# Attention opening of a fused kernel: two queues for the first heads' rows, four buffers for the first values, six pairs three slots sooner, ones in pieces

## The reference

```python
# attention: 16 heads of 16, causal, no bias
q, k, v = Wq x, Wk x, Wv x            # x after layernorm
attn = softmax(where(causal, q k / sqrt(16), -inf))
x = x + layernorm(Wo (attn v))
# mixture of experts: 8 experts, 2 of them per token
logits = router x + bias              # x after layernorm
gate, up = split(gate_up x + bias)    # 512 each
act = (clip(up) + 1) * min(gate, 7) * sigmoid(1.702 min(gate, 7))
x = x + layernorm(sum over 2 experts of weight * (down act + bias))
```

## Time and profile before

| | before |
|---|---|
| median of 3 runs | 2109.95 us (2108.41 to 2113.77) |
| the profiled execution | 2107.62 us, of which span 2105.9 |
| TensorE busy | 1964.5 us, 93% |
| VectorE busy | 1588.1 us, 75% |
| ScalarE busy | 1338.4 us, 64% |
| GpSimd busy | 948.3 us, 45% |
| granted TensorE clock, mean | 0.975 |

### The profile page before, as it was taken

The page is one execution under the profiler, slowest core; times in us unless marked ns, Lnnn a source line. Parts: engine busy times, 40 slices in busy tenths (PEclk is TensorE's granted clock), DMA queues, the critical chain, the costliest instruction groups (busy, mean ns, idle before and its releaser), DMA issues. The chain is left out here.

```text
span 2105.9 us, 50512 instructions
## 1 busy us (share of the span) xinstructions
PE 1964.5 (93%) x13630; PEld 1301.5 (62%) x13631; DVE 1588.1 (75%) x5427; ACT 1338.4 (64%) x3413; POOL 948.3 (45%) x1442
## 2 busy tenths in 40 slices
PE   6799999999999999999999999999999999999970
PEld 4334444444444444444433349999999999999970
DVE  2877788888888888887888827778767777777757
ACT  3377777777777777777777675555444444444436
POOL 5233344455646556456455563455323333333327
PEclk9799999999999999999999999999999999999995
DMA  7533546464454635545355368889788888887867
GB/s 210 184 112 126 176 156 199 134 208 160 155 167 138 193 126 168 164 138 180 118 171 182 113 205 255 234 246 252 219 249 256 259 261 256 256 258 234 242 183 319
DMA packets 259201, 413.99 MB, mean 197 GB/s; under 512 B 37056, under 2 KB 195264, under 8 KB 251840
## 3 DMA queue, kind: packets, MB, share of 16 engines
q1 hardware_dynamic: 219392, 367.28, 53.1%
q0 software_dynamic: 29824, 35.54, 9.6%
q10 hardware_dynamic: 9792, 8.93, 1.4%
HBM read 288.64 MB, written 122.41 MB: 195 GB/s over the span
## 5 line engine op out<-in xcount | busy, mean ns | idle before, releaser
L1013 ACT ACTIVATE arena<-ps_e 128x512 f32<-128x512 f32 (+3 forms) x1536 | 687.3, 493 | 276.4 <-PE ps_e L1233 260.0
L648 DVE CUSTOM_DVE_ANT_0 arena<-ps_s,c 128x128 bf16<-128x128 f32 (+3 forms) x1024 | 479.1, 481 | 61.0 <-PE ps_s L1214 57.1
L1214 PE MATMUL ps_s<-arena 96*128 96x512 bf16 (+3 forms) x1536 | 489.3, 334 | 25.4 <-DMA arena<-qk_parts 7.1
L1233 PE MATMUL ps_e<-arena 98*128 98x512 bf16 (+3 forms) x1536 | 483.2, 329 | 2.9 <-ACT arena L1013 2.0
L651 DVE TENSOR_REDUCE cmax<-ps_s 128x1 f32<-128x512 f32 x512 | 351.2, 686 | 142.7 <-PE ps_s L1214 132.5
L1367 PE MATMUL ps_s<-arena 128*128 128x128 f32 x3296 | 405.2, 276 | 6.5 <-DMA arena<-in_gate_up 4.9
L1367 PEld LDWEIGHTS ps_s<-arena 128*128 128x128 f32 x3296 | 394.3, 192 | 19.1 <-DMA arena<-in_gate_up 7.9
L1214 PEld LDWEIGHTS ps_s<-arena 96*128 96x128 bf16 x1536 | 152.1, 101 | 356.7 <-DVE cmax L648 91.5
L1252 PE MATMUL ps_o<-arena 128*32 128x512 f32 (+3 forms) x3072 | 329.9, 502 | 4.9 <-ACT ot L1027 3.5
L545 POOL TENSOR_SCALAR_AFFINE_SELECT arena<-arena 128x512 f32<-128x512 f32 x256 | 162.9, 636 | 294.8 <-ACT arena L1013 294.4
L529 POOL DMA_INDIRECT acc<-blank,place_now x136 | 216.2, 1590 | 132.0 <-POOL place_now L524 67.6
(11 more groups left out here) (179 smaller groups left out, 2796.9 us busy)
## 6 DMA issues: line engine op xcount, KB each, us to landing
arena<-in_gate_up SPq DMA_DIRECT2D x138, 1024.0 KB
arena<-qk_parts SPq DMA_DIRECT2D x384, 128.0 KB, 2.9
qk_parts<-space SPq DMA_DIRECT2D x120, 192.0 KB
d_xin<-xs SPq DMA_DIRECT2D x141, 130.5 KB
v_aug<-space SPq DMA_DIRECT2D x32, 512.0 KB, 4.9
arena<-v_aug SPq DMA_DIRECT2D x32, 512.0 KB
o_t<-ot SPq DMA_DIRECT2D x64, 256.0 KB, 2.0
c_x<-in_x SPq DMA_DIRECT2D x34, 256.0 KB, 5.4
```

The lines of the kernel that those rows point to most:

```text
L648: dve.tensor_tensor_reduce(summed[:, m % RJ, 0:w], ps_s[:, m % RS, 0:w], after[:, HALF - w:HALF], 1.0, LOWEST, ALU.add, ALU.max, dst).then ...
L1013: act.activation(pw[:, n % RP, 0:w], ps_e[:, n % RE, 0:w], ACT.Exp, scale=SCALE).then_inc(e_done, 1)
L1214: pe.matmul(ps_s[:, m % RS, 0:w], qs[0:ROWS, slot, i * P:(i + 1) * P], ks[0:ROWS, slot, k0:k0 + w], start=True, stop=True).then_inc(s_scor ...
L1233: pe.matmul(ps_e[:, n % RE, 0:w], ks[0:ROWS_M, slot, j * P:(j + 1) * P], qs[0:ROWS_M, slot, q0:q0 + w], start=True, stop=True).then_inc(e_ ...
```

## The change

Four edits. The rows of quad 0 are issued by SyncE (q) and ScalarE (k), both in slot `BEGIN`; all quads' rows now go q first, then k. Pairs 2 and 3 get value buffers of their own in the arena, which VectorE fills with ones beforehand. The first pairs are placed in earlier slots. The two rows of ones are filled in three pieces, one per quad buffer.

| slot of | before | after |
|---|---|---|
| turning of pairs 0 to 5 | -36, -33, -30, -27, -23, -16 | -39, -36, -33, -30, -27, -20 |
| values copy of pairs 0 to 5 | -22, -21, -20, -19, -17, -10 | -27, -26, -25, -24, -21, -14 |
| `qk_parts` store of pairs 0 to 5 | -29, -26, -23, -20, -16, -9 | -32, -29, -26, -23, -17, -13 |
| load of x for pairs 4 to 7 | -31, -28, -24, -17 | -34, -31, -28, -21 |
| value stores of pairs 0 to 3 | -18 | -18 |
| ones | -18 | -20, -12, -9 |
| pair 6 and later | | the same |

```diff
-    A_AT = [BEGIN - 18 + 3 * a for a in range(EARLY)] + [BEGIN - 5, BEGIN + 2] + [NE * (a - 6) - 4 for a in range(6, PAIRS)]
-    V_AT = [BEGIN - 4 + a for a in range(EARLY)] + [start + 6 for start in A_AT[EARLY:]]
+    A_AT = [BEGIN - 21 + 3 * a for a in range(EARLY + 1)] + [BEGIN - 2] + [NE * (a - 6) - 4 for a in range(6, PAIRS)]
+    V_AT = [BEGIN - 9 + a for a in range(EARLY)] + [start + 6 for start in A_AT[EARLY:]]
...
+        def vout_of(a):
+            if 2 <= a < EARLY:
+                return arena[:, 13312 + (a - 2) * 1024:13312 + (a - 1) * 1024].rearrange("p (s c h d) -> p s c h d", s=4, c=2, h=4)
+            return vout[:, a % 2]
...
+        def load_rows(engine, quad, w):
+
+            b, s, u = quad // 4, quad % 4, quad % SETS
+            for nth, part in enumerate(((0, 0, 0, 1, 1, 2), (0, 1, 2, 0, 1, 0))[w]):
+                engine.dma_start((qs, ks)[w][nth:ROWS:ROWS // DH, u * 4:u * 4 + 4].rearrange("r h t -> r (h t)"),
+                                 qk_v[b, w, s // 2, s % 2, part]).then_inc(loads[u], 16)
...
-                for a in pairs_due(7, 9, g):
+                for a in due([max(start + (7 if a < FIRST_EVEN else 9), BEGIN + 1 if a >= EARLY else SLOTS.start) for a, start in enumerate(A_AT)], 0, g):
...
                 if g == BEGIN:
                     for u in range(2):
                         sp.wait_ge(qk_out[u], EARLY // 2 * Q_STORES * 16)
-                    load_heads(0)
+                    load_rows(sp, 0, 0)
                     for a in range(EARLY):
                         store_values(a)
...
-                if g == BEGIN:
-                    pool.wait_ge(a_p3, 2 * EARLY + 1)
-                    pool.memset(ks[ROWS:ROWS_M], -1.0).then_inc(ones, 1)
-                    pool.wait_ge(ones, 1)
+                for u, (at, done_by, n) in enumerate(((BEGIN - 2, a_p3, 2 * EARLY + 2), (BEGIN + 6, a_p3, 2 * EARLY + 4), (BEGIN + 9, s_mlo, 2))):
+                    if g == at:
+                        pool.wait_ge(done_by, n)
+                        pool.memset(ks[ROWS:ROWS_M, u * 4:u * 4 + 4], -1.0).then_inc(ones, 1)
+                        pool.wait_ge(ones, u + 1)
...
-            dve.memset(vout, 1.0).then_inc(v_ones, 1)
+            dve.memset(vout, 1.0)
+            dve.memset(arena[:, 13312:15360], 1.0).then_inc(v_ones, 1)
...
+                if g == BEGIN:
+                    for u in range(2):
+                        act.wait_ge(qk_out[u], EARLY // 2 * Q_STORES * 16)
+                    load_rows(act, 0, 1)
...
                             act.wait_ge(a_v, a + 1)
-                            if a >= 2:
+                            if a >= EARLY:
                                 act.wait_ge(v_out[u], a // 2 * 16)
...
-                    pe.wait_ge(ones, 1)
+                    pe.wait_ge(ones, SETS)
```

More of the change, by code:

```diff
@@ L323, in load_heads @@
             def load_heads(quad):
[L325 to L333, removed]
+                load_rows(sp, quad, 0)
+                load_rows(sp, quad, 1)
             def load_values(quad):
@@ L341, in store_values @@
                 sp.dma_start(v_aug[b, :, :, 2 * j:2 * j + 2].rearrange("s p c h d -> p s (c h d)"),
-                             vout[:, u].rearrange("p s c h d -> p s (c h d)")).then_inc(v_out[u], 16)
+                             vout_of(a).rearrange("p s c h d -> p s (c h d)")).then_inc(v_out[u], 16)
             def slots(j):
@@ L1106, in _ @@
                             for t in range(2):
-                                last = act.activation(vout[:, u, :, t, :, 0:DH],
+                                last = act.activation(vout_of(a)[:, :, t, :, 0:DH],
                                                       bank[:, t * D:(t + 1) * D].rearrange("p (s h d) -> p s h d", s=4, h=4), ACT.Copy)
```

## The result

| | before | after |
|---|---|---|
| median of 4 runs | 2110.01 us (2108.41 to 2113.77) | 2131.98 us (2128.35 to 2135.08) |
| the profiled execution | 2107.62 us, span 2105.9 | 2128.35 us, span 2126.6 |
| granted TensorE clock, mean | 0.975 | 0.970 |

The ratio is 1.0101, with a 95% interval of 1.0083 to 1.0119: the change costs 22 us (17.5 to 25). That is slower, as forecast, but 13 us more than the 2119 forecast and 5 above the range's end.

A forecast was written before the change was run, and what follows sets the result against it. The opening, with its 13 us gap before the head phase, was taken to shift everything behind it; +11.7 and -1.5 make +10.2, giving 2117.8 from the profiled execution or 2120.1 from the median, taken as 2119 us, range 2110 to 2127.

The forecast's parts named there:

- Steps 1 to 3: Opening before the head rows: TensorE 2.7 us late, pair 3's store landed at 46.8, SyncE's rows from 48.0, 6.1 later.
- step 2: Pair 3's store: ScalarE's second part done at 41.1, third part at 42.3 instead of 37.4, landed at 46.8.
- step 3: SyncE before its head rows: pair 7's x waits for pair 5's normalising at 47.6; rows start at 48.0, not 41.91.
- Step 4: ScalarE's copy of pair 4's values waits for the stores of pairs 0 and 2, until 58.0, ahead of its row loads.
- Step 5: ScalarE's six rows: issued from 60.3 over 3.2 us, landing 2.8 later; first score 66.3 against 51.74, bounds 62.9 to 70.
- The rule weighed in step 5: ScalarE's rows: a second issuing engine saves only initiation time, the 16 DMA engines being shared; at most some 3.4 us gained.
- Step 6: Head phase: VectorE starts at 66.6, 11.7 us later than 54.9; the phase of 43.1 us gets 1.5 shorter.
- rival C: No change: short value landings, cheap ScalarE issues, a head phase losing its 6.7 us idle; +1 to +4, 2110; chance 0.10.
- The sum: Whole kernel: +11.7 us for the later start and -1.5 in the head phase give +10.2.
- A: Intended gain: values wait and half the issues go, rows land at 47.9; -8.2 us, 2099 to 2102, say 2100; chance 0.08.
- B: Partial delay: SyncE starts near 42 to 43 but ScalarE still waits at its copy; +5 us, 2114; chance 0.12.
- The sign that had 0.78: Whole kernel: slower by over 0.3% (6.3 us) given 0.78, faster 0.09, within 0.3% 0.13.

The follow-up runs named there:

- e8: The kernel before with the four value buffers alone (rows q before k, one queue, old slots): 2106.71 us, ratio 0.9997.
- e12: The kernel after with value stores of pairs 0 to 3 one slot behind each copy and all quad 0 rows on SyncE: 2114.21 us, ratio 1.0024.
- e2: The kernel after with all twelve rows of quad 0 on SyncE: 2117.99 us, ratio 1.0053.
- e3: The kernel after with the value stores of pairs 0 to 3 one slot behind each copy, still two queues: 2114.52 us, ratio 1.0039.
- e4: The kernel after with SyncE waiting for all of quad 0 before issuing the rows of quads 1 and 2: 2124.29 us, ratio 1.0081.
- e7: The kernel after with old slots and ones in one piece, value stores issued only when quad 0 has landed: 2108.23 us, ratio 0.9997.
- e5: The kernel after with 28 unused matmuls on TensorE before the first score: 2124.90 us, ratio 1.0078.
- e1: The kernel after with the slots of before and the ones in one piece; two queues and four buffers stay: 2110.38 us, ratio 1.0018.
- e6: The kernel before with only the ones filled in three pieces: 2108.57 us, ratio 1.0005.
- e10: The kernel before with four value buffers, 36 unused matmuls and pair 7's x loaded right behind the value stores: 2104.07 us, ratio 0.9986.

## Why the prediction was right in kind and wrong in size

The runs make a ladder to the exponent score: before 98.2; four buffers 96.1 (e8); the new slots with the ones in pieces, the stores early and one queue 101.5 (e12, 5.4 us more); the stores back in slot -18, so that ScalarE waits and TensorE with it, 108.4 (e2, 6.9 more); the k rows put behind that wait 116.2 (after, 7.8 more). The second queue costs nothing where ScalarE is not held (e3, 101.0) and 7.8 us where it is.

**Steps 1 to 3** held: GpSimd finished pair 3's third part at 42.95 (forecast 42.3), and SyncE's rows began at 47.18 (48.0). Some of this nearness is luck: ScalarE was done with the second part at 40.1 and not 41.1, but GpSimd had pair 5's scale and shift ahead of the third part, which step 2 left out, and began it at 41.8. The load of x for pair 7, which step 3 had as the last wait, was not it: issued at 46.27 in 0.37 us, it left 0.5 us in which SyncE waited on, by its order for the stores of pair 3 (forecast landed at 46.8). The slots without the wait cost 5.1 us at the first score (e12's 57.2 against e8's 52.1), where these steps had 6.1 for the start of the rows.

**Step 4** held: the wait was there, in one piece of 11.30 us, on pair 2's store, released at 57.55 (58.0). 15.2 of the 18.0 us hang on it (e3): 6.9 by the wait with no row behind it (e2 against e12), and the rest by the rows behind it.

**Step 5** failed at its last term, the time of ScalarE's six rows beside SyncE's. ScalarE began at 59.47, 0.8 us before the forecast 60.3. Its six issues then spread over 4.7 us and not 3.2, and the landing behind them took 6.5 us and not 2.8: the first score at 70.7 and not 66.3, past the upper bound of 70 as well. The forecast had nothing for SyncE's passing rows and its upper bound 1.5 us; they took 5.2 (70.7 - 59.5 - 3.2 - 2.8), and e4, which removes just these rows, has the landing of 2.7 us back. The bound took these loads at 369 GB/s; with the engines full they passed at 225 to 262. The rule weighed in step 5 (the Trainium skill, DMA: Bandwidth & Descriptors, "Issuing engines are not separate DMA queues") agrees with these traces: e7 and e3 have the first score within 0.5 us of their counterparts with one queue (e8 and e12). I had used it to cap a gain and not to price the loss of a load that must share the engines with one that has time.

**Step 6** failed in its sign for the head phase: -1.5 us forecast, +1.9 measured (43.3 to 45.2, just over the 45 us that the prediction named as its test). It had pair 5's work in the first slots at half clock and set no loss for it. In the first 16 us behind the first row maximum the granted clock is 0.65 where the kernel before has 0.80, and VectorE gets 10.7 us of work done instead of 12.8. e5 shows the clock to cost 4.0 us: with the unused matmuls the phase from the first score is 41.5 us. A long stand of TensorE does not by itself explain the clock: in e1 it stands for 12.2 us ahead of the first score (11.6 and 8.5 us in the kernel after, with pair 5's first work between) and has 0.90 in the first 16 us, against 0.64. Why the clock stayed low for longer in the kernel after is open. The trace of before had the sign of it, in the earlier trace rows; I had used it against rival C only.

**The sum**: +11.7 for the start was +16.1, and -1.5 was +1.9; 10.2 + 4.4 + 3.4 = 18.0. The other 4 us, to the 22 us of the medians, are in no stage that I could name; 18.0 lies within the 17.5 to 25 of the interval. All edits costed at nothing (ones, fills, row order) were: e6, and e8 with its second fill, show no loss.

**The rivals.** A's time, 2100, came nowhere. Its mechanism was tried without its obstacle: with the buffers and two queues and no wait of ScalarE (e1, e7) the first score does not come before 51.7, not the 48 that it supposes. Of its 3.2 us saving of issues 1.0 is left in e7 (last issue at 47.9, before at 48.91), since the rows on ScalarE begin 3 us behind SyncE's, behind a copy; and the score then stands 3.7 us behind that issue, not 2.8. B and C needed less than the forecast, and the loss was more. The sign that had 0.78 came. The range was too narrow, as it had no room for a head phase longer than before's.

**Open.** Why only 2.0 of e4's 3.6 us arrived, and why its clock was 0.61, was not separated. The 3 us of the tail, and the 4 us between the exponent scores and the medians, have no cause shown. The copy of pair 4 with a semaphore for pair 0's store alone was not tried.

## What to carry to other kernels

A buffer wait that an edit removes is to be looked for in the next user of the buffer: here it came back at pair 4, the next user of pair 0's buffer, since the copies moved four to five slots and the stores that free the buffers did not. It was worth some 7 us by itself, as TensorE's next work stood behind the copy, and some 8 more because DMA issues had been put behind it on the same engine. An engine that computes was a poor issuer here for a load that is waited for: its list is held by semaphores that have nothing to do with the load. Before a second queue is used, ask what share of the DMA engines one queue already takes for this form of transfer (0.67 here), and what else will be in flight, as urgent rows are slowed by rows with time to spare.

## What the runs showed of the hardware

The 128 KB row loads take 0.59 us to issue on SyncE and 0.61 on ScalarE, with nothing saved on the latter; the 0.35 us of the earlier trace rows belongs to another load. Under load one issue took 2.1 us. Landing took 2.6 us in the median and 3.0 at most in e4, where SyncE issues no other rows beside the k rows; it took up to 6.3 beside another queue's rows (after) and 7.1 beside value stores and another queue (e1). Issuing holds ScalarE up: in e1 its next instruction behind the six rows begins after 5.83 us without work, in e7 after 3.31.

The first heads' rows in the kernel before, on one queue, from 44 to 49.5 us:

```profile
44.00:49.50 5.50, 0.61 (x3) 0.19 (x1) 0.00 (x0) 0.00 (x0) 5.50 (x1) 0.84 0.67 212
```

One queue thus passes 212 GB/s at a share of 0.67, and two at shares of 0.95 to 1.09 no more than 225 to 271 (after, e3): the rate per share falls when both are in flight.

The head phase went with the granted clock of its first 16 us and not with that of the whole. In these 16 us VectorE gets 10.1 us of work done at 0.61 (e4), 10.5 at 0.64 (after), 11.5 and 11.6 at 0.79 (e3, e12), 12.7 at 0.81 (e8), 13.9 at 0.90 (e1), 13.2 at 0.93 (e2) and 14.0 at 0.97 (e5). Behind them it is idle for 2.7 to 3.3 us in after, e1, e2, e3, e5 and e12, at clocks from 0.55 to 0.80, and for 4.4 and 3.9 us in e4 and e8. With four buffers VectorE's busy time is 36.4 to 36.8 us throughout. My reading is that VectorE sets the phase at full clock, and that at half clock TensorE's work at the start of the phase leaves it too little room. e5 tests this directly; e10 against e8 agrees (44.0 to 41.1 us with unused matmuls, of which the load of x, for which e8 waits 0.76 us, is a small part).
